# Experts' rows padded to 128 in place of 256: each half of a 256-row tile has its own expert

## The reference

```
probs = softmax(t @ W_gate + b_gate)
topv, topi = top_k(probs, 2)
topv = topv / sum(topv)
mid  = relu(einsum('nd,edh->neh', t, W1) + b1)      # 256 -> 1024
eout = einsum('neh,ehd->ned', mid, W2) + b2         # 1024 -> 256
out  = (sum over the two of topv * eout) @ W_out + b_out
x + out
```

## Time and profile before

| | |
|---|---|
| median of 3 runs | 658.56 us (655.08 to 660.2) |
| span of the profiled execution | 659.3 us |
| granted TensorE clock, mean over it | 0.915 |
| PE busy | 548.1 us, 83% |
| PEld busy | 484.3 us, 73% |
| DVE, ACT, POOL busy | 392.4, 286.1, 245.0 us |

### The profile page before, as it was taken

How to read it: one execution, slowest core, us unless ns; L and a number is a source line. 1 busy time by engine, 2 the same in 40 slices (tenths; PEclk the granted TensorE clock), 3 DMA queues, 4 the chain that set the end, 5 groups by cost and what they waited for, 6 DMA issues and landing times.

```text
span 659.3 us, 14861 instructions
## 1 busy us (share of the span) xinstructions
PE 548.1 (83%) x4527; PEld 484.3 (73%) x4528; DVE 392.4 (60%) x704; ACT 286.1 (43%) x504; POOL 245.0 (37%) x244
## 2 busy tenths in 40 slices
PE   0898920222899999999999999999999999992887
PEld 0797820211698989999898989898989898981665
DVE  4687589994455555555555555555555555642754
ACT  2688683203444444444444434343434343521443
POOL 1022116987224343434342424242424242316700
PEclk9899675555799999999999999999999999996899
DMA  6789644200111111111111111111111111148585
GB/s 200 262 299 320 191 160 130 86 0 26 38 34 49 50 48 48 48 48 48 48 48 48 49 46 52 44 55 40 56 40 56 40 54 41 48 140 291 174 284 181
DMA packets 39467, 64.55 MB, mean 98 GB/s; under 512 B 5844, under 2 KB 27158, under 8 KB 39318
## 3 DMA queue, kind: packets, MB, share of 16 engines
q1 hardware_dynamic: 30678, 39.64, 18.7%
q0 software_dynamic: 8768, 24.65, 11.7%
HBM read 45.66 MB, written 18.61 MB: 97 GB/s over the span
## 4 chain that ended last, share of the span: by engine, by line
PE 74%; DVE 10%; DMA 8%; issue 4%; ACT 2%; SPq 2%; POOL 1%; ACTq 0%; DVEq 0%; POOLq 0%
PE bank L1004 31%; PE bank L989 11%; PE bank L990 11%; PE bank L991 11%; DMA w1s<-y_by_choice 3%; PE bank L908 3%; DMA region<-in_x 3%; PE bank L970 3%; DVE w1s L782 2%; DVE w1s L785 1%; PE bank L904 1%; PE bank L1034 1%; DVE w1s L860 1%; DMA region<-z_by_token,src 1%; POOL oha L415 1%
## 5 line engine op out<-in xcount | busy, mean ns | idle before, releaser
L559 ACT ACTIVATE region<-bank,b1p,cbits 128x256 f32<-128x256 f32 x312 | 158.9, 559 | 243.5 <-PE bank L991 168.4
L1004 PE MATMUL bank<-w2s,region 128*128 x1872 | 210.6, 273 | 0.0
L1004 PEld LDWEIGHTS bank<-w2s,region 128*128 128x128 f16 x1872 | 183.2, 98 | 20.8
L444 POOL DMA_INDIRECT y_by_choice<-region,dst x78 | 83.0, 1064 | 252.2 <-DVE region L822 240.1
L989 PE MATMUL bank<-region,w1s 128*128 128x256 f16 x624 | 172.2, 276 | 4.5 <-DVE region L811 4.5
L990 PE MATMUL bank<-region,w1s 128*128 128x256 f16 x624 | 172.2, 276 | 0.0
L991 PE MATMUL bank<-region,w1s 128*128 128x256 f16 x624 | 172.0, 276 | 0.0
L832 DVE CAST region<-region 128x512 f16<-128x512 f32 x156 | 68.7, 440 | 144.3 <-ACT region L559 133.7
L834 DVE TENSOR_TENSOR region<-region 128x512 f16<-128x512 f32 x156 | 108.0, 692 | 5.4
L437 POOL DMA_INDIRECT region<-z_by_token,src x78 | 80.1, 1026 | 30.6 <-issue 23.0
L989 PEld LDWEIGHTS bank<-region,w1s 128*128 x624 | 61.8, 99 | 12.9 <-issue 5.1
(11 more groups left out here) (175 smaller groups left out, 527.9 us busy)
## 6 DMA issues: line engine op xcount, KB each, us to landing
region<-in_L_ffn_W SPq DMA_DIRECT2D x16, 1024.0 KB, 6.8
w1s<-y_by_choice SPq DMA_DIRECT2D x16, 512.0 KB, 4.4
region<-in_x SPq DMA_DIRECT2D x8, 512.0 KB, 7.8
z_by_token<-w1s POOLq DMA_DIRECT2D x16, 256.0 KB, 5.4
w1s<-in_x SPq DMA_DIRECT2D x4, 1024.0 KB
out<-w1s SPq DMA_DIRECT2D x16, 256.0 KB, 2.9
region<-z_by_token,src POOLq DMA_INDIRECT x78
y_by_choice<-region,dst POOLq DMA_INDIRECT x78
```

The lines of the kernel that those rows point to most:

```text
L444: g.indirect_dma_start(out=ybuf, out_offset=bass.IndirectOffsetOnAxis(ap=at, axis=0), in_=ysb[:, a % 2, h, :], in_offset=None).then_inc(s_ ...
L559: m = s.activation(midf[:, b, c * TS:(c + 1) * TS], FB[b][:, c * TS:(c + 1) * TS], ACT.Relu, bias=b1p[:, bass.ds(e, 1), f:f + 1].rearrange ...
L1004: last = mm(YB[par][:, h * D:(h + 1) * D], mids[:, par, l, b, c * TS + h * P:c * TS + (h + 1) * P], w2_at(e, w, f), start=(f == 0 and l == ...
```

## The change

Each expert's block of slots is now padded to a multiple of P = 128 slots, and a tile of 256 slots has one expert for each of its halves. The worst case is 71 halves, rounded up to 36 tiles (NA = 72). `tile_e` has an entry for each half, and each place that read one expert reads two. In the first layer each half has its own three matmuls per k, with 128 columns streamed in place of 256. In the second layer the number and width of the matmuls stay, but the weights that stream are now those of the half's expert. ScalarE's relu is issued per half. The loop covers tiles 4 to 33, and tiles 34 and 35 are written out.

```diff
-    NTILE = (K * N + E * (TS - 1)) // TS
+    NTILE = -(-((K * N + E * (P - 1)) // P) // H)
...
-            with eng.Fori(2, NTILE // 2) as j:
+            with eng.Fori(2, NTILE // 2 - 1) as j:
                 step(j * 2, 0, j)
                 step(j * 2 + 1, 1, j)
-            step(NTILE - 1, 0, NTILE // 2)
+            for a in range(NTILE - 2, NTILE):
+                step(a, a % 2, a // 2)
...
-                e = act.value_load(tile_e[0:1, bass.ds(a, 1)], min_val=0, max_val=E - 1)
+                es = [act.value_load(tile_e[0:1, bass.ds(a * H + h, 1)], min_val=0, max_val=E - 1) for h in range(H)]
...
-                        m = s.activation(midf[:, b, c * TS:(c + 1) * TS], FB[b][:, c * TS:(c + 1) * TS], ACT.Relu,
-                                         bias=b1p[:, bass.ds(e, 1), f:f + 1].rearrange("p e c -> p (e c)"),
-                                         scale=cbits[:, 0, 1, bass.ds(e, 1)].bitcast(f32))
+                        for h, e in enumerate(es):
+                            o = slice(c * TS + h * P, c * TS + (h + 1) * P)
+                            m = s.activation(midf[:, b, o], FB[b][:, o], ACT.Relu,
+                                             bias=b1p[:, bass.ds(e, 1), f:f + 1].rearrange("p e c -> p (e c)"),
+                                             scale=cbits[:, 0, 1, bass.ds(e, 1)].bitcast(f32))
...
                     for c in range(2):
-                        o = FB[b][:, c * TS:(c + 1) * TS]
-                        for k in range(KD):
-                            w = w1_at(e, 0, k, 2 * b + c)
-                            mm(o, w, xs[:, par, 0, k, :], start=(k == 0), stop=False)
-                            mm(o, w, xs[:, par, 1, k, :], start=False, stop=False)
-                            last = mm(o, w1_at(e, 1, k, 2 * b + c), xs[:, par, 0, k, :], start=False,
-                                      stop=(k == KD - 1))
+                        for h, e in enumerate(es):
+                            t = slice(h * P, (h + 1) * P)
+                            o = FB[b][:, c * TS + h * P:c * TS + (h + 1) * P]
+                            for k in range(KD):
+                                w = w1_at(e, 0, k, 2 * b + c)
+                                mm(o, w, xs[:, par, 0, k, t], start=(k == 0), stop=False)
+                                mm(o, w, xs[:, par, 1, k, t], start=False, stop=False)
+                                last = mm(o, w1_at(e, 1, k, 2 * b + c), xs[:, par, 0, k, t], start=False,
+                                          stop=(k == KD - 1))
...
                         for l, w in ((0, 0), (1, 0), (0, 1)):
-                            for h in range(H):
+                            for h, e in enumerate(es):
                                 last = mm(YB[par][:, h * D:(h + 1) * D],
                                           mids[:, par, l, b, c * TS + h * P:c * TS + (h + 1) * P], w2_at(e, w, f),
...
-            def expert(a):
-                return pe.value_load(tile_e[0:1, bass.ds(a, 1)], min_val=0, max_val=E - 1)
+            def experts(a):
+                return [pe.value_load(tile_e[0:1, bass.ds(a * H + h, 1)], min_val=0, max_val=E - 1) for h in range(H)]
```

More of the change, by code:

```diff
@@ L118, in moe_program @@
         src = sb("src", [P, 2, NA], i32)
-        tile_e = sb("tile_e", [1, NTILE], i32)
-        te = sb("te", [1, 2, NTILE, E], f32)
+        tile_e = sb("tile_e", [1, NA], i32)
+        te = sb("te", [1, 2, NA, E], f32)
         zss = sb("zss", [P, NT // 2], f32)
@@ L752, in _ @@
                                       tot[:].rearrange("p e t -> p (e t)"), 0.0, ALU.mult, ALU.add))
-            link(v.tensor_scalar(cnti[:, 0, :], incl[:, :, NT - 1], float(TS - 1), None, ALU.add))
-            link(v.tensor_scalar(cnti[:, 1, :], cnti[:, 0, :], TS.bit_length() - 1, None, ALU.logical_shift_right))
+            link(v.tensor_scalar(cnti[:, 0, :], incl[:, :, NT - 1], float(P - 1), None, ALU.add))
+            link(v.tensor_scalar(cnti[:, 1, :], cnti[:, 0, :], P.bit_length() - 1, None, ALU.logical_shift_right))
             link(v.tensor_copy(cnt[:, 0, :], cnti[:, 1, :]))
@@ L757, in _ @@
             link(v.tensor_tensor(cnt[:, 2, :], cnt[:, 1, :], cnt[:, 0, :], ALU.subtract))
-            link(v.tensor_scalar(cnt[:, 3, :], cnt[:, 2, :], float(TS), None, ALU.mult))
+            link(v.tensor_scalar(cnt[:, 3, :], cnt[:, 2, :], float(P), None, ALU.mult))
             link(v.tensor_tensor(sv[:], incl[:], tot[:], ALU.subtract))
@@ L800, in _ @@
                             ALU.logical_shift_right).then_inc(s_idx, 1)
-            link(v.tensor_tensor(te[:, 0], bc(iota_row[0:1, 0:NTILE].unsqueeze(2), [1, NTILE, E]),
-                                 bc(cnt[0:1, 1, :].unsqueeze(1), [1, NTILE, E]), ALU.is_ge))
+            link(v.tensor_tensor(te[:, 0], bc(iota_row[0:1, 0:NA].unsqueeze(2), [1, NA, E]),
+                                 bc(cnt[0:1, 1, :].unsqueeze(1), [1, NA, E]), ALU.is_ge))
             link(v.tensor_reduce(te[:, 1, :, 0], te[:, 0], AX.X, ALU.add))
@@ L815, in y_out @@
             def y_out(a, par, before):
-                e = dve.value_load(tile_e[0:1, bass.ds(a, 1)], min_val=0, max_val=E - 1)
+                es = [dve.value_load(tile_e[0:1, bass.ds(a * H + h, 1)], min_val=0, max_val=E - 1) for h in range(H)]
                 dve.wait_ge(s_yp, a + 1)
@@ L844, in _ @@
             tiles(dve, tile)
-            y_out(NTILE - 1, 0, NTILE // 2)
+            y_out(NTILE - 1, (NTILE - 1) % 2, (NTILE - 1) // 2)
             def finish(i, par):
@@ L978, in w2_at, with first_layer @@
                 return w2s[:, bass.ds(e, 1), l, c, :].rearrange("p e f -> p (e f)")
-            def first_layer(a, par, e):
+            def first_layer(a, par, es):
                 pe.wait_ge(s_xl, a + 1)
@@ L1008, in second_layer @@
                 last.then_inc(s_yp, 1)
-            def expert(a):
-                return pe.value_load(tile_e[0:1, bass.ds(a, 1)], min_val=0, max_val=E - 1)
+            def experts(a):
+                return [pe.value_load(tile_e[0:1, bass.ds(a * H + h, 1)], min_val=0, max_val=E - 1) for h in range(H)]
             def tile(a, par, j):
-                first_layer(a, par, expert(a))
+                first_layer(a, par, experts(a))
                 if not isinstance(a, int) or a < NTILE - 1:
@@ L1017, in tile @@
                 if later(a, 1):
-                    second_layer(a - 1, 1 - par, expert(a - 1))
+                    second_layer(a - 1, 1 - par, experts(a - 1))
             rows_t(0, 0, 0)
@@ L1025, in _ @@
             tiles(pe, tile)
-            second_layer(NTILE - 1, 0, expert(NTILE - 1))
+            second_layer(NTILE - 1, (NTILE - 1) % 2, experts(NTILE - 1))
             def project(i, par):
```

2 lines of the change are left out of this document (1 added, 1 removed).

## The result

The kernel after takes 822.2 us (median of 4 runs, 820.6 to 825.6) against 657.6 of the kernel before beside it: a ratio of 1.251, 95% interval 1.246 to 1.256. The forecast was 813 us in a range of 785 to 885. Its profiled execution spans 819.1 us, 159.8 more than that of before; the expert stage alone is 597.1 us where it was 432.8, 164.3 more. The stage explains all of it.

The account below looks back on a forecast made before the run. PE's sequencer, making weight addresses and loading experts, was taken to bound each tile at 16.4 us: 659.3 - 432.8 + 36 x 16.4 + 2 - 4 - 1 = 814, less 0.7 from profile to median: 813 us, range 785 to 885.

Parts of the forecast that it names:

- The bound before: Expert tiles before the change: the array sets the pace at 10.9 us a tile, hiding the sequencer's 9.2.
- The tile's 16.4 us: Expert tile after the change: sequencer-bound, 9.2 + 4.0 + 2.0 + 1.5 less 0.3, 5.4 above the array's need.
- The array's 0.055: First layer: each 128-column matmul takes about 0.055 us in the array, making a tile's array time 11.0 us.
- Rivals B: Array also slow, at the fp32 transposes' pace: perhaps 17 us a tile interleaved, 835 us in all; 10%.
- C (0.082): Sequencer's price half counted, array at 0.082 us per first-layer matmul: 13.5 us a tile, 711 us; 3%.
- E, no address kept: Second layer needs 48 addresses a tile, adding 2.0 us a tile: 885 us; 6%.
- D, the clock: Idle array gets half clock for half the time, + 2.8 us a tile: 915 us; 8%, half with smaller loss.
- F, the loop fetched again: Tile loop's larger body outgrows what is held; 15 passes each wait 2.4 us, + 36: 849 us; 4%.
- The sum around the tile: Whole span: profiled 659.3 less the 432.8 stage, plus 36 x 16.4, + 2 - 4 - 1, giving 814 us.
- my estimate for the ends: Stage's ends: second tile's wait and longer load + 2 us; six written-out tiles without branch, constant waits, - 4.
- Outside the stage I took 1 us off: Setup: one-hot products shrink from 78 to 72 columns, expert table grows by under 0.5 us; net - 1.

Follow-up runs that it names:

- the second layer was shared: Kernel after, with both halves of a tile taking second-layer weights from the first half's expert, 16 fewer addresses a tile: 780.0 us, ratio 1.187.
- the last run: Kernel after with two addresses per instruction, expert numbers loaded once, and four first-layer address instructions ahead of twelve matmuls: 634.2 us, ratio 0.967.
- paired kernel: Kernel after, with two weight addresses computed by one register instruction, 48 in place of 96 a tile, matmuls untouched: 774.5 us, ratio 1.180.
- paired kernels with bursts: Kernel after with two addresses per instruction, 774.5 us; the same with expert numbers also loaded once and kept, 710.7 us.
- one-expert run: Kernel after, with both halves of a tile using the first half's expert weights in both layers, 48 addresses a tile: 652.5 us, ratio 0.993.

## Why the prediction was right

**The bound before** holds: taking sequencer work away from the kernel before changes nothing (657.8), adding it costs 122 us.

**The tile's 16.4 us** came out as 16.67 in the mean of the loop. By the sequencer's own parts in the tile at 403.2 us, whose first address is at 403.2, the last of the first layer at 411.7, the second layer's at 413.4 and 417.6, and the next tile's at 419.8:
```profile
L993 PEldq FUSED_REGOPS  x32: 46/46/46, 403.2 to 411.5; - x32
...
L995 PEldq FUSED_REGOPS  x32: 46/46/46, 403.3 to 411.7; - x32
...
L1008 PEldq FUSED_REGOPS  x32: 46/46/51, 413.4 to 417.6; - x32
...
L993 PEldq FUSED_REGOPS  x1: 46/46/46, 419.8 to 419.8; - x1
```
The first layer is 8.5 (forecast 8.2), up to the second layer 1.7 (1.95), second layer 4.2 (4.2), to the next tile 2.2 with the branch (2.05 in the mean). The 0.3 too few in the first layer is the pause. It disappeared with wide relus on ACT (9 us of 822), and also with narrow relus when the second layer was shared. So ACT's time as such is hidden, as forecast, and the sum lacked a stop of PE whose cause is open.

**The array's 0.055** per matmul of 128 columns, an estimate from a half-clock row and half of 0.109, is 0.056 in the last run (5.31 us from a first layer's first matmul to its 96th). Rivals B (the array as slow as the transposes) and C (0.082) fall. The Trainium skill, "TensorE: Matmul & The Clock Gate", section "Back-to-back issue gap", gives about 81 ns for a load and matmul of 128 columns; the measurement, 56 ns with a load each, decides. The first layer of the paired kernel does average 0.080 (7.7 us for 96), but in bursts and pauses, not at an even pace, and the last run's, without bursts, takes 5.3.

**E, no address kept** in the second layer, is refuted by 32 a tile. **D, the clock,** by 0.99 in the stage; it did fall, for parts of the stage, in the paired kernels with bursts. **F, the loop fetched again:** q8 brought 17 packets and 0.28 MB with 15 passes, against 11 and 0.18. That alone could be a packet a pass, but the packets come before the loop and in its first pass. Nine came from 158.7 to 244 us; from there to 720 us, some 14 passes, there is none on q8 and one on the other instruction queue (packets, MB, share, of either stretch):
```profile
q8 instruction: 9, 0.15, 0.8%
```
```profile
q14 instruction: 1, 0.01, 0.0%
```
So a body of some 835 instructions on PE is held over the branch.

**The sum around the tile** was right partly by luck. For the profiled span it gave 814 us against 819.1. The other 4 of the 9 us between 813 and 822.2 lie between a profiled run and the median: the one of the kernel before lay 0.7 us above its median, that of the kernel after 3.1 below. In the span two misses stood against each other. The stage was forecast at 588 us and took 597.1, and 36 x 0.27, 10 us, are the tile's. I had also put 36 tiles in the place of the whole stage and so dropped the 7 us of start and last drain that the first paragraph had named. With them my estimate for the ends would have been 5 us more than 36 tiles; without them it was 2 less, and measured are 3 less (36 x 16.67 is 600.1), mostly because the first two tiles take 12.2 and 15.7 us. Outside the stage I took 1 us off, and it became 4.5 us shorter; the stages of the runs with the same setup began anywhere between 157.6 and 167.4 us, so this is no effect of the change that these runs can show.

**What the model lacked** did not show in this sum. I added up the sequencer's time for a whole tile and set it against the array's for a whole tile.
Left untried: the kernel before with 36 tiles and 256-row padding, as its worst case needs 39. The worth of fewer tiles shows in the last run all the same: 36 x 11.13 against 39 x 10.92 is 25 us, and 22 were measured.

## What to carry to other kernels

A matmul whose weights lie at a run-time address pays the sequencer for each new address; count addresses, not matmuls, before halving a tile, and set sequencer against array stage by stage. If the sequencer loses, the repair may be cheap: two addresses in one register instruction, registers kept over a tile, and the addresses of a group computed ahead of its matmuls turned 822 us into 634. When a chain of waits has no clear owner and says "issue", look at the sequencer's rows before any engine's.

## What the runs showed of the hardware that I had not expected

- A FUSED_REGOPS that makes two addresses takes 74 ns and a step of 0.153 us, one that makes one takes 46 ns and a step of 0.124: the second address costs 0.03 us.
- PE's sequencer made its last second-layer address 1.9 us, some 18 matmuls, ahead of the last weight load in the one-expert run and in that with the second layer shared, and 2.25 us in the last run, where six matmuls stand behind the last address instruction and not two. It never had a whole second layer in the queue.
- With one pair instruction ahead of each three matmuls PE stopped after some 78 first-layer matmuls and went on in bursts 0.7 us apart, which costs 2.3 to 2.4 us a tile; with four such instructions ahead of twelve matmuls, never (13.6 and 11.1 us a tile). Tiles without gathers had no bursts in either order.
- A milder form, one stop of some 0.4 us a tile, is in the kernel after. It went when ACT's relus were half as many, and also when the second layer's addresses were, while the 0.7 us bursts stayed under either change.
- ACT was released 2.4 to 2.6 us after the recorded start of the matmul that it waited for, with bursts (415.0 and 417.6) and without (312.59 and 314.96, the kernel before); in the last run it is 0.5 us (408.80 and 409.27).
- A loop body of some 835 instructions on PE ran for 14 passes without a packet on q8.
